# A two-axis Toeplitz layer on one core: opening steps and stores reordered, convolution units taken in pairs with the transposed v copied by VectorE, and the norms of the second half in one chain

## The reference

```python
xn = srms(x)                                  # x / (norm(x) / sqrt(96) + 1e-8), by token
u = jax.nn.silu(xn @ u_w.T + u_b)             # 96 -> 288
v = jax.nn.silu(xn @ v_w.T + v_b)             # 96 -> 288
# tno: a small network (256 wide, 3 layers) gives 2*64 - 1 coefficients per channel;
# v is convolved with them along one axis (a Toeplitz matrix of 64 x 64 per channel)
out = tno(v, -3, rpe2...) + tno(v, -2, rpe1...)
out = u * out
return out @ o_w.T + o_b + x
```

## Time and profile before

| | |
|---|---|
| median of 3 runs | 791.74 us (791.65 to 794.81) |
| the profiled execution | 791.33 us, its span 789.5 us |
| TensorE matmul busy | 749.0 us, 95% of the span |
| VectorE, ScalarE, GpSimd busy | 472.1, 533.4, 280.7 us |
| chain of waits that ended last | PE 84%, DMA 6%, DVE 4%, ACT 2% |
| granted TensorE clock, mean | 0.981 |

### The profile page before, as it was taken

One profiled execution on the slowest core, in us unless ns is written; L12 is line 12 of the kernel. 1 busy time (PEld: TensorE's weight loads), 2 busy tenths in 40 slices (PEclk: granted clock), 3 DMA queues, 4 the chain that ended last, 5 costly groups with the idle time before them and its releaser, 6 DMA issues.

```text
span 789.5 us, 19225 instructions
## 1 busy us (share of the span) xinstructions
PE 749.0 (95%) x7148; PEld 676.6 (86%) x7148; DVE 472.1 (60%) x860; ACT 533.4 (68%) x866; POOL 280.7 (36%) x187
## 2 busy tenths in 40 slices
PE   3799989998999999899999999998999999899997
PEld 3799878997999999799999999997999999787785
DVE  7666643336888888444444444444544444388886
ACT  2366656765666666677777777774666666676775
POOL 4333333212221122455555455521000000289984
PEclk9699998999999999999999999999999999999999
DMA  8655563369978986488888988959655555589995
GB/s 196 164 167 164 163 126 146 150 206 204 203 172 189 194 187 159 134 255 271 272 269 269 270 271 268 271 191 212 145 135 134 134 131 131 170 256 324 338 337 182
DMA packets 132049, 161.11 MB, mean 204 GB/s; under 512 B 69516, under 2 KB 97164, under 8 KB 131980
## 3 DMA queue, kind: packets, MB, share of 16 engines
q1 hardware_dynamic: 131980, 160.15, 72.5%
HBM read 109.49 MB, written 50.63 MB: 203 GB/s over the span
## 4 chain that ended last, share of the span: by engine, by line
PE 84%; DMA 6%; DVE 4%; issue 2%; ACT 2%; POOL 1%; SPq 1%; ACTq 0%; POOLq 0%; DVEq 0%
PE ps L992 25%; PE ps L1074 16%; PE ps L1046 10%; PE ps L1059 9%; PE ps L1002 9%; PE ps L1012 9%; PE ps L983 3%; DMA x_e<-in_x_eT 3%; PE ps L1015 1%; DMA stage<-a_dram 1%; DVE x_e L903 1%; DMA u_dram<-u_in 1%; PE ps L966 1%; DMA u_dram<-u_out 1%; DVE g L894 1%
## 5 line engine op out<-in xcount | busy, mean ns | idle before, releaser
L509 POOL TENSOR_TENSOR u_in<-u_in,v 128x1152 f32<-128x1152 f32 (+2 forms) x66 | 174.2, 2644 | 155.7 <-DMA u_in<-u_dram 139.4
L894 DVE TENSOR_TENSOR g<-ps,g 128x512 fp32r<-128x512 f32 (+1 forms) x192 | 125.4, 679 | 49.6 <-ACT g L576 40.4
L850 DVE COPY toepB<-stage 64x512 f32<-64x512 f32 x144 | 107.5, 747 | 79.3 <-PE ps L1074 71.2
L1074 PE MATMUL ps<-toepB,vt 128*128 128x128 f32 x1152 | 141.8, 277 | 0.6 <-POOL toepB L493 0.6
L1074 PEld LDWEIGHTS ps<-toepB,vt 128*128 128x128 f32 x1152 | 136.4, 194 | 0.9 <-POOL toepB L493 0.7
L992 PE MATMUL ps<-wv,xh 97*128 97x288 f32 x512 | 122.0, 314 | 6.5 <-ACT u_in L553 4.1
L992 PE MATMUL ps<-wu,xh 97*128 97x288 f32 x512 | 124.8, 309 | 2.1
L761 DVE TENSOR_TENSOR xl<-ps,xh 96x512 fp32r<-96x512 f32 x64 | 43.9, 687 | 136.2 <-ACT xh L549 136.2
L553 ACT ACTIVATE v<-ps 128x576 f32 (+1 forms) x128 | 83.4, 652 | 39.2 <-PE ps L992 29.7
L1002 PE MATMUL ps<-ident,u_in 128*128 128x128 f32 (+1 forms) x768 | 101.4, 276 | 4.5 <-POOL u_in L509 4.5
L1012 PE MATMUL ps<-g,wo 128*96 128x512 f32 x384 | 101.9, 400 | 0.0
(11 more groups left out here) (81 smaller groups left out, 1010.0 us busy)
## 6 DMA issues: line engine op xcount, KB each, us to landing
stage<-a_dram SPq DMA_DIRECT2D x144, 256.0 KB, 4.3
u_in<-u_dram SPq DMA_DIRECT2D x64, 576.0 KB, 5.6
u_dram<-u_out SPq DMA_DIRECT2D x48, 576.0 KB, 3.3
x_e<-in_x_eT SPq DMA_DIRECT2D x64, 192.0 KB, 4.4
out<-x_e SPq DMA_DIRECT2D x64, 192.0 KB, 4.2
u_dram<-u_in SPq DMA_DIRECT2D x16, 576.0 KB, 2.8
x_n<-in_x SPq DMA_DIRECT2D x16, 384.0 KB, 5.6
xa<-in_x SPq DMA_DIRECT2D x64, 96.0 KB, 4.7
```

Source lines behind the costliest of these rows:

```text
L509: return nc.gpsimd.tensor_tensor(out=tile, in0=tile, in1=v[:, start // 2:end // 2, bass.ds(t * NB, NB)].rearrange("p c n e -> p n c e"), o ...
L850: nc.vector.tensor_copy(toepB[n % 2][rows, :, rows], stage[n % STAGES][rows, axis].rearrange("p k c -> p c k")[:, :, ::-1]).then_inc(toepB ...
L894: nc.vector.tensor_tensor(out=low, in0=ps[0:w, bank], in1=high.bitcast(f32), op=ALU.subtract).then_inc(gl_ready, 1)
L1074: last = nc.tensor.matmul(ps[:, SET_BANK[n % 2] + c // NB, (c % NB) * P:(c % NB + 1) * P], vt[n % 2][:, c], toepB[n % 2][:, c], start=Fals ...
```

## The change

1. **Opening.** TensorE runs 30 transposes of the identity before its first step (`WARM`). The high parts of the weights are made by ScalarE instead of VectorE; the low part of the second one, and the low part of x of step 0, come behind the sum of squares of steps 1 to 3 on VectorE. GpSimd puts its squares of chunk 2 one step later. The first `rpe_part` (the network's sum) moves behind the projections of step 1, and VectorE's first `rpe_square` and `sum_a0(1)` behind `low_x` of step 1.
2. **Stores of the coefficients.** The two DMAs of `store_a` become nine parts of two, one part behind each `store_u` of steps 16 to 24. The first stages are loaded one step earlier, behind a wait for all parts.
3. **Pairs.** TensorE takes the columns of units n and n + 1, then rows of n, transposes for n + 2, rows of n + 1, transposes for n + 3. `vt` is copied by VectorE. VectorE makes toepA of n + 2 and of n + 3 one after the other, before toepB of n + 2.
4. **Norms of the second half.** The eight sums go side by side into a buffer `n_half` of 128 columns; the chain runs once, at units 30 to 33. GpSimd's scaling and the load of one u tile wait for that one chain.

```diff
@@ store_a (SP)
-            def store_a():
+            def store_a(part):
                 sp.wait_ge(a_ready, 2)
+                units = slice(A_UNITS * part, A_UNITS * (part + 1))
...
@@ phase_a (SP)
-                    if last and r == 2:
-                        sp.wait_ge(a_stored, 32)
+                    if last and r == 1:
+                        sp.wait_ge(a_stored, 32 * A_PARTS)
...
                     store_u(0, CH * c + r, u_tile(0, r), ua_stored[r % 2])
+                    part = CH * (c - LAYERS - 1) + r
+                    if 0 <= part < A_PARTS:
+                        store_a(part)
@@ phase_a (GpSimd)
-                        for k in ((), (0,), (1,), (2, 3))[r]:
+                        for k in (((), (), (0,), (1, 2, 3)) if first else ((), (0,), (1,), (2, 3)))[r]:
                             square_a0(c + 2, k)
@@ phase_c (ScalarE)
-                evacuate_vt(0)
                 for n in range(UNITS):
-                    if n:
-                        evacuate_y(n - 1)
-                    if n + 1 < UNITS:
-                        evacuate_vt(n + 1)
...
+                    evacuate_y(n)
+                    if half == 0 and n == UNITS - 2:
                         high_x(STEPS, 0)
@@ sums and norms (VectorE)
             def sum_a1(j):
-                sum_squares(CH, x_n[:], 1 + CHUNKS + j, CH * CHUNKS + j)
+                dve.wait_ge(squared, CH * CHUNKS + j)
+                nc.vector.reduce_sum(n_half[:, 0, CH * NB * j:CH * NB * (j + 1)], x_n[:], axis=AX.X).then_inc(norms_summed, 1)
...
-            def norms_a1(j):
-                return norms(STEPS + CH * j, CH, 1 + CHUNKS + j)
+            def norms_a1():
+                return norms(STEPS, STEPS, 1 + CHUNKS, tile=n_half)
@@ phase_c (VectorE)
+                def evacuate_vt(n):
+                    N = UNITS * half + n
+                    dve.wait_ge(vt_transposed, N + 1)
+                    wait(dve, conv_done, N - 1)
+                    nc.vector.tensor_copy(vt[n % 2][:], ps[:, VT_BANK:VT_BANK + 2].rearrange("p b (c m) -> p (b c) m", m=P)
+                                          ).then_inc(vt_ready, 1)
...
                 for n in range(UNITS):
-                    if n + 2 < UNITS:
-                        dve.wait_ge(columns_done, TILES * (UNITS * half + n + 1))
-                        toeplitz(0, n + 2)
+                    for k in range(2):
+                        if n % 2 == 0 and n + k + 2 < UNITS:
+                            dve.wait_ge(columns_done, TILES * (UNITS * half + n + k + 1))
+                            toeplitz(0, n + k + 2)
                     if half == 0 and n % 4 == 2 and n // 4 < CHUNKS:
                         sum_a1(n // 4)
-                        pieces = iter(norms_a1(n // 4))
-                    if half == 0 and n >= 2:
+                        pieces = iter(norms_a1())
+                    if half == 0 and n >= 4 * CHUNKS - 2:
                         run(itertools.islice(pieces, 4))
                     if n + 2 < UNITS:
                         dve.wait_ge(conv_done, UNITS * half + n + 1)
                         toeplitz(1, n + 2)
+                        evacuate_vt(n + 2)
@@ opening and phase_a (TensorE)
+            for _ in range(WARM):
+                nc.tensor.transpose(ps[:, O_BANK, 0:P], ident[:], ident[:])
             transpose_x(0, 0)
...
-                    if isinstance(c, int) and c <= LAYERS:
+
+                    networks = isinstance(c, int) and c <= LAYERS
+                    if networks and not (first and r < 2):
                         rpe_part(c, r)
                     if not start:
                         for pair in range(PAIRS):
                             project(t, r, pair)
+                    if first and r == 1:
+                        rpe_part(0, 0)
@@ phase_c (TensorE)
-                transpose_v(0)
-                for n in range(UNITS):
-                    if n < 2:
-                        pe.wait_ge(silu_done, PAIRS * STEPS * (half + 1) - 1 + n)
-                    along_columns(n)
-                    if n + 1 < UNITS:
-                        transpose_v(n + 1)
...
+                for n in range(2):
+                    transpose_v(n)
+                    pe.wait_ge(silu_done, PAIRS * STEPS * (half + 1) - 1 + n)
+                for n in range(0, UNITS, 2):
+                    for k in range(2):
+                        along_columns(n + k)
+                    for k in range(2):
+                        along_rows(n + k)
+                        if n + 2 + k < UNITS:
+                            transpose_v(n + 2 + k)
+                        elif half == 0 and k == 0:
+                            transpose_x(STEPS, 0)
```

More of the change, by code:

```diff
@@ L125, in x_chunk @@
             return x_late[c - FREE_CHUNKS - 1][:]
+        n_half = place("n_half", [P, 3, STEPS * NB], V + 13824)
         x_n = place("x_n", [P, CH * NB, E], V + 22528)
@@ L207, in tno_kernel @@
         columns_done, conv_done, conv_out = sem("columns_done"), sem("conv_done"), sem("conv_out")
+        WARM = 30
+        A_UNITS = 4
+        A_PARTS = UNITS // A_UNITS
         RPE_LOADS = 1 + 2 * (RC + RC + 1)
@@ L366, in phase_c @@
                     load_u(half, k, k)
+                if half == 0:
+                    sp.wait_ge(norms_ready, CHUNKS + 2)
                 sp.wait_ge(columns_done, TILES * (UNITS * half + UNITS - 1))
@@ L451, in scale_a0, with scale_a1 @@
                 scale(t, x_chunk(c)[:, NB * r:NB * (r + 1)], r)
-            def scale_a1(t, loads, chunk, r):
-                pool.wait_ge(norms_ready, CHUNKS + chunk + 2)
+            def scale_a1(t, loads, r):
+                pool.wait_ge(norms_ready, CHUNKS + 2)
                 pool.wait_ge(xa_loaded[r % 2], 32 * loads)
@@ L502, in _ @@
             for t in range(2):
[L503 removed]
+                scale_a1(t, 1, t)
             def gate(half, t, r, loads, start=0, end=D):
@@ L576, in high_g @@
                     nc.scalar.copy(tile[2 * w:3 * w, 4], ps[0:w, bank]).then_inc(gh_ready, 1)
+            act.wait_ge(weights_loaded, 4 * 16)
+            for n, w in enumerate((wv, wu)):
+                nc.scalar.copy(w[:, 0].rearrange("p (h q) -> p h q", h=NCH), rows(W_RAW + NCH * n, NCH, E, slice(0, KE))
+                               ).then_inc(w_split, 1)
             high_x(0, 0)
@@ L594, in phase_c @@
             def phase_c(half):
-                def evacuate_vt(n):
-                    N = UNITS * half + n
-                    act.wait_ge(vt_transposed, N + 1)
-                    wait(act, conv_done, N - 1)
-                    nc.scalar.copy(vt[n % 2][:], ps[:, VT_BANK:VT_BANK + 2].rearrange("p b (c m) -> p (b c) m", m=P)
-                                   ).then_inc(vt_ready, 1)
                 def evacuate_y(n):
@@ L683, in _, with norms @@
                 set_x_rows(k)
-            def norms(first_step, steps, batch, layer=None):
+            def norms(first_step, steps, batch, layer=None, tile=n_tmp):
                 cols = steps * NB
                 wide = cols if layer is None else cols + 2
-                total, root, inv = (n_tmp[:, k, 0:wide] for k in range(3))
+                total, root, inv = (tile[:, k, 0:wide] for k in range(3))
                 small = [lambda: nc.vector.tensor_scalar(total[:, 0:cols], total[:, 0:cols], 1.0 / E, None, ALU.mult)]
@@ L696, in piece @@
                     if k == 0:
-                        dve.wait_ge(norms_summed, batch + 1)
+                        dve.wait_ge(norms_summed, batch + 1 if tile is n_tmp else 1 + 2 * CHUNKS)
                         if layer is not None:
@@ L772, in _, with split_low @@
             run(norms(0, 1, 0))
-            dve.wait_ge(weights_loaded, 4 * 16)
-            for n, w in enumerate((wv, wu)):
-                raw = rows(W_RAW + NCH * n, NCH, E, slice(0, KE))
-                high, low = (w[:, k].rearrange("p (h q) -> p h q", h=NCH) for k in range(2))
-                nc.vector.tensor_copy(high, raw).then_inc(w_split, 1)
-                dve.wait_ge(w_split, 2 * n + 1)
-                nc.vector.tensor_tensor(out=low, in0=raw, in1=high.bitcast(f32), op=ALU.subtract).then_inc(w_split, 1)
-                if n == 0:
-                    dve.wait_ge(x_all_loaded, 32)
-                    square_x(CH - 1).then_inc(squared, 1)
-                    low_x(0, 0)
+            def split_low(n, w):
+                dve.wait_ge(w_split, n + 1)
+                nc.vector.tensor_tensor(out=w[:, 1].rearrange("p (h q) -> p h q", h=NCH),
+                                        in0=rows(W_RAW + NCH * n, NCH, E, slice(0, KE)),
+                                        in1=w[:, 0].rearrange("p (h q) -> p h q", h=NCH).bitcast(f32), op=ALU.subtract
+                                        ).then_inc(w_lows, 1)
+            split_low(0, wv)
+            dve.wait_ge(x_all_loaded, 32)
+            square_x(CH - 1).then_inc(squared, 1)
             dve.wait_ge(squared, CH - 1)
```

(6 more changed lines are left out.)

23 lines of the change are left out of this document (7 added, 16 removed).

## The result

The changed kernel takes 818.1 us (median of 4 runs, 816.11 to 819.37), the kernel before 791.69 in the same session (790.65 to 794.81). The ratio is 1.0338, 95% interval [1.0313, 1.0363]: slower by 3.4%, 26.4 us. The forecast was 808, with 786 to 824 as its range. The profiled execution took 819.37 us, its span is 817.5 us.

What follows compares the result with a forecast made beforehand. TensorE was taken to bound both convolutions, with late stages slowing the first after the change. From 791.3 us: opening +1.0, stores -6.3, first convolution +24, second -2.2, giving 808 us; stated range 786 to 824.

Steps and rivals of the forecast that it cites:

- The ring of stages: First convolution: late stage requests close a loop per pair; four units (a four) take 18.5 us, not 16.05: +17 us.
- The fit on VectorE: Convolution pairs: VectorE's copies, vt included, need 6.5 us of a 7.65 us pair; fits barely in the second convolution.
- GpSimd beside VectorE: First convolution: GpSimd's square delays toepA by up to 0.7 us per four units; +5 us in the range.
- Start of C0: First convolution's start: vt(0) and toepB(2) wait for other copies and stage 3, delaying the columns of unit 2: +3.5 us.
- End of C0: First convolution's end, units 30 to 33: the single 128-column norm chain takes 6.8 us of VectorE, 3.8 free: +3 us.
- Stores: Coefficient stores in part A: nine parts remove TensorE's 4.1 us idle and 2.2 us of half clock: -6.3 us.
- Opening: Kernel opening: nothing gained or lost by the new order, +1.0 us for the clock; bounds -2 to +4.
- the clock's term: Opening, step after the spread: may run at low clock after TensorE's wait, 2.2 us more at even odds.
- What pairs save: TensorE in both convolutions: 64 x 64 tiles entered and left once per pair, saving 0.38 us; a pair takes 7.65.
- C1: Second convolution: seventeen pairs save 6.4 us, its start costs 3.6 plus 0.6 for low clock: -2.2 us.
- The rival of a falling clock: First convolution: waits in pairs drop TensorE's clock, ten falls of 2.2 us each: 830 us; chance 0.10.
- The two faster rivals: First convolution: stages land in time, 781 us, chance 0.15; or partly, 16.4 us per four units, near 792, chance 0.08.

Runs made afterwards that it cites:

- e4: Changed kernel with the vt copies back on ScalarE, pairs and toepA order as changed: 811.17 us, ratio 1.0266.
- e1: Changed kernel with toepA of the odd unit made late again, just ahead of its own toepB: 802.67 us, ratio 1.0168.
- e2: Changed kernel with the two x_n loads issued behind stage 4j + 3 instead of ahead of it: 818.91 us, ratio 1.0356.
- e3: Changed kernel with the sum over x_n put behind toepB and vt instead of between toepA and toepB: 858.39 us, ratio 1.0864.
- e12: Changed kernel with toepA of the odd unit late again and the second half's squares left out: 796.19 us, ratio 1.0067.
- e6: Kernel before with only the coefficient stores cut in nine parts, first stages loaded where they were: 783.34 us, ratio 0.9902.
- e10: Kernel before plus stores in parts, pairs, toepA late, vt on ScalarE behind all of v, odd units' transposed v in banks 6 and 7: 779.45 us, ratio 0.9869.
- e11: Changed kernel with x_n loads behind stage 4j + 3 and the second half's squares left out: 811.97 us, ratio 1.0279.

## Why the prediction was right, and where it was off

**The ring of stages (+17): right as to the cause, nearly right in size.** Fours were put at 18.5 us; from the columns of unit 2 to those of unit 30 they are 18.9 (18.8 from unit 6 on). e4 and e1 show the cause from two sides: take the load from VectorE and the waits stay on the stages, put toepA back and 17 us go. What was wrong is the make-up: I had the sum in one turn (8.8) and x_n in the other (9.7); the queue has both in one (10.8) and none in the other (7.3). The sum of the two is nearly the same, 18.1 against 18.5, so the forecast held while e2 and e3, which rest on the make-up, missed.

**The fit on VectorE: right for C1 by load, not by order; too easy for C0.** In C1 VectorE is busy 110 of 137 us, yet its vt copies come 0.2 us late in each pair. For C0 the prediction kept VectorE's time apart from the ring. e1 and e12 show that without the ring it would have been the next bound: 17.2 us a four with the squares beside it, 16.0 without.

**GpSimd beside VectorE: in the range, as said.** In the changed kernel a square stretched one toepA copy by up to 0.4 us, no more (1.04 to 1.09 in place of 0.65). In the orders of e1 and e2 it cost up to 2.5 us a time. The open question, whether a copy out of PSUM escapes, is answered below.

**Start of C0 (+3.5): mis-sized.** Counted from the transposes of step 31, the columns of unit 2 were to begin 24.7 us later and began 27.4 us later: stage 3 came 9.6 us behind the issue of x_n (9.0 assumed), its toepA took 1.04 us beside the square, and the transposes ahead ran at the low clock, 1.98 us. **End of C0 (+3): +3.8.** The wide chain is as costed (a reciprocal of 128 columns 0.95 us, as reckoned), but vt copies and toepB stand between its parts; the last two pairs take 11.0 and 10.1 us. In C0 these give 2.7 + 2.7 (fours) + 0.8 = 6.2 us, where +29.4 exceeds the forecast's terms, 17 + 3.5 + 3 = 23.5, by 5.9.

**Stores (-6.3): right**, -6.3 by the table, and 7 by e6 (6.1 in its trace between the same marks). **Opening (+1.0): mis-sized**, +3.3. The step that failed is the clock's term, 2.2 us at even odds: the low clock cost 2.2 us on the matmuls and 0.8 on the spread, and the order, put at nothing, 0.3. VectorE's chain is 2 us longer than estimated, but the projections ahead of it ended 2 us earlier; that the spread came on time is luck.

**What pairs save (0.38): right as TensorE's need, not reached.** By the lines under e10 TensorE needs 7.66 us for a pair, 0.37 less than before. The make-up was off: leaving saves 0.2 and not 0.28, since eight transposes take 0.95 us and not 0.88; entering saves about 0.15 and not 0.10. That the two errors cancel is luck. What failed is the step that a pair takes what TensorE needs: it saved 0.13 in C1 as changed, where the wait is for vt from VectorE, and 0.2 in e10, where it is most likely for v from ScalarE. The Trainium skill, page TensorEngine Tiling (Array Packing), section Key Properties, says that a change of tiling mode drains TensorE; here leaving costs about 0.2 us and entering about 0.15.

**C1 (-2.2): mis-sized**, +1.6. Its columns begin 5.7 us later than before against the rest of the program (3.6 + 0.6 forecast), in 10 us of low clock, and pairs take 7.90 and not 7.65, which saves 2.1 us in all and not 6.4. From the columns of the last pair on it takes 2.1 us less than before, which no term foresaw and no run explains. e4 shows the cause of the start: with vt on ScalarE it is back at 17.6 us.

The rival of a falling clock was small: the granted clock fell five times in C0, for 3.4 us each, at 174, 187, 208, 300 and 320 us; in the kernel before it fell once there, at 190 us. The two faster rivals needed stages that land in time.

## What to carry to other kernels

Where a ring of buffers is refilled from work on an engine, write down for each step who must have finished before the next refill can be *asked for*, in the order of the queues: moving one copy ahead of another turned a slack of three units into a loop within a pair. An engine that looks loaded may only be late; take load off it and see whether its waits grow. And two bounds of nearly the same length hide each other: removing one can show almost nothing (e2), so remove both before calling the first one harmless. The same holds for what an order saves: e10 and the changed kernel each lose about half of what pairs save on TensorE to a copy that comes late, on two different engines.

## What the runs showed of the hardware

- A VectorE copy out of PSUM wasn't held up by GpSimd; a copy from SBUF to SBUF was, where GpSimd had begun first. In e2, GpSimd squared from 206.59 to 209.57 us. Of the three VectorE copies in that time the vt copy out of PSUM kept its 1.23 us, and toepA from SBUF took 1.57 instead of 0.65:

```profile
206.59 2.98 POOL L469 TENSOR_TENSOR x_n<-x_n 128x1536 f32<-128x1536 f32 x1 [21.71 <-DMA x_n<-in_x]
```

```profile
206.98 1.23 DVE L864 COPY vt<-ps 128x1024 f32<-128x1024 f32 x1
208.49 1.57 DVE L849 COPY toepA<-stage 128x512 f32<-128x512 f32 x1 [0.29 <-DMA stage<-a_dram]
```

  GpSimd's 2.98 us, where a square alone takes 2.75, begin while a toepB copy runs (from 206.29, 0.65 us): the copy that had begun first kept its time. Two more vt copies that lie wholly within squares in e2 kept 1.23 us too. The Trainium skill, page SBUF — State Buffer, section Who interferes with whom, says that a VectorE instruction with at most one SBUF input, outside the two-port modes, doesn't contend with GpSimd; the 1.23 us agree.
- Transposes of a constant alone raised the clock. In the changed kernel TensorE did nothing else from 2.14 us on; they start 0.213 us apart up to 6.25 us and 0.109 apart from there, the ratio of the two levels, 1.2 and 2.4 GHz. The gain didn't last: TensorE had no work from 9.9 to 13.5 us, and the granted clock was at the low level again from 13.1 to 19.9 us, so that the first projections, from 13.54 us on, ran at it.
- The two DMAs of a stage asked for by itself landed 3.8 and 4.2 us after their issue in C0 of the changed kernel (at 224.86 and 225.47 us); in e11 the two asked for right behind x_n took 7.2 and 7.4 us. The DMA engines' mean share of 0.66 in C0 doesn't show that.
